# Routed experts that begin after five images' dispatch, with their weights turned inside the MLP and the expert loop written out

## What is computed

```python
h2 = layer_norm(x, norm2_g, norm2_b)
m = gelu(h2 @ W1.T + b1) @ W2.T + b2        # 128 -> 512 -> 128
x = x + m
flat = _ln_t(x)                              # norm again, 8192 x 128
topk_probs, topk_idx = top_k(softmax(flat @ router_w.T), 2)      # 8 experts
h = silu(flat @ w1[e].T) * (flat @ w3[e].T)                      # 128 -> 341
out = sum over the two chosen e of gate * (h @ w2[e].T)
x = x + out
```

## Time and profile before

| what | value |
|---|---|
| median of 3 executions | 1099.61 us (1098.13 to 1100.76) |
| the profiled execution | 1101.17 us, span of the core 1099.4 us |
| blocks up to the MLP | 0 to 427 us |
| MLP steps | 427 to 671 us |
| slot table, rest of the dispatch | 671 to 709 us |
| experts' weights turned | 709 to 724 us |
| expert block, first load to last scatter | 725 to 1054 us |
| last block | to 1099.4 us |
| busy | PE 832.1 (76%), DVE 664.2, ACT 445.1, POOL 447.2 us |
| mean granted clock of PE | 0.886 |

### The profile page before, as it was taken

One profiled execution on the slowest core, in us unless ns is written; L12 is line 12 of the kernel. 1 busy time (PEld: TensorE's weight loads), 2 busy tenths in 40 slices (PEclk: granted clock), 3 DMA queues, 4 the chain that ended last, 5 costly groups with the idle time before them and its releaser, 6 DMA issues. The chain is left out here.

```text
span 1099.4 us, 21202 instructions
## 1 busy us (share of the span) xinstructions
PE 832.1 (76%) x5345; PEld 678.7 (62%) x5346; DVE 664.2 (60%) x2221; ACT 445.1 (40%) x1173; POOL 447.2 (41%) x486
## 2 busy tenths in 40 slices
PE   2798987579999994995667643169998999999920
PEld 1233332468888873884656642159898989888820
DVE  3498887557777755573444233436666666666658
ACT  1233331466666542652443311254343343333335
POOL 0010100255777771035445556404444434444335
PEclk9899999789999996997777755589999999999965
DMA  5010000000000002001012112112111111111159
GB/s 134 25 39 20 19 0 1 1 1 1 2 1 2 2 1 78 25 21 36 30 35 88 40 39 69 48 25 59 57 57 55 58 58 58 58 55 56 58 162 320
DMA packets 60857, 51.99 MB, mean 47 GB/s; under 512 B 9644, under 2 KB 54148, under 8 KB 60804
## 3 DMA queue, kind: packets, MB, share of 16 engines
q1 hardware_dynamic: 41792, 29.49, 9.5%
q0 software_dynamic: 8448, 17.45, 4.4%
q10 hardware_dynamic: 10564, 4.41, 1.4%
HBM read 28.63 MB, written 22.69 MB: 47 GB/s over the span
## 5 line engine op out<-in xcount | busy, mean ns | idle before, releaser
L1646 POOL DMA_INDIRECT mixed<-yt,sidx x136 | 130.2, 957 | 219.7 <-ACT yt L1746 120.9
L1412 POOL DMA_INDIRECT xs<-hx,didx x128 | 124.2, 970 | 152.3 <-DVE didx L1498 107.2
L1695 PE MATMUL bank<-w2T,hmt 128*128 (+1 forms) x816 | 113.3, 275 | 0.0
L559 DVE TENSOR_TENSOR res<-bank,norm 128x512 f32<-128x512 f32 x144 | 95.2, 686 | 25.0 <-PE bank L389 23.2
L1757 DVE TENSOR_TENSOR hm<-bank,sl 128x342 f32<-128x342 f32 x138 | 71.1, 515 | 58.4 <-ACT sl L1728 49.2
L1746 ACT ACTIVATE yt<-bank 128x128 f32<-128x128 f32 x136 | 37.8, 278 | 160.4 <-PE bank L1695 156.7
L1695 PEld LDWEIGHTS bank<-w2T,hmt 128*128 128x128 f32 (+1 forms) x816 | 101.7, 191 | 0.0
L1333 PE MATMUL bank<-downT,mgv 128*128 128x128 f32 x512 | 76.8, 312 | 16.3 <-issue 16.2
L1688 PE MATMUL bank<-cst,hm 128*128 128x128 f32 (+1 forms) x411 | 68.2, 275 | 22.3 <-DVE hm L1757 13.5
L1333 PEld LDWEIGHTS bank<-downT,mgv 128*128 128x128 f32 x512 | 72.3, 225 | 18.8 <-issue 18.5
L458 POOL TENSOR_TENSOR redu<-redu_full,redu 32x512 fp32r<-32x512 f32 x16 | 20.2, 1276 | 148.5 <-ACT redu L432 148.5
(11 more groups left out here) (285 smaller groups left out, 2119.7 us busy)
## 6 DMA issues: line engine op xcount, KB each, us to landing
xg<-xs SPq DMA_DIRECT2D x144, 65.0 KB, 1.8
y<-mixed SPq DMA_DIRECT2D x16, 512.0 KB, 4.8
stage<-in_x SPq DMA_DIRECT2D x8, 512.0 KB, 3.8
out<-tok ACTq DMA_DIRECT2D x16, 256.0 KB, 5.0
mixed<-yt,sidx POOLq DMA_INDIRECT x136, 2.3
raw<-in_L_ffn_w SPq DMA_DIRECT2D x16, 128.0 KB
xs<-hx,didx POOLq DMA_INDIRECT x128
res<-in_L_ffn_w SPq DMA_DIRECT2D x1, 1364.0 KB
```

Of the source, the lines that this page charges most:

```text
L559: dve.tensor_tensor(prod[t].rearrange("p (h w) -> p h w", w=SIDE), tapb[g % TB][:, :].rearrange("p (h w) -> p h w", w=SIDE), norm[s][:, 16 ...
L1412: pool.indirect_dma_start(xs, bass.IndirectOffsetOnAxis(didx[b % NX][:, j, k:k + 1], 0), hx[b % NX][:, j, :], None).then_inc(dispatched[b ...
L1646: pool.indirect_dma_start(mixed, bass.IndirectOffsetOnAxis(sidx[s][:, :], 0), yt[s][:, :], None).then_inc(scattered[s], 16)
L1695: ins = pe.matmul(yb[r % 2][:, 0:P], hmt[r % 2][0:m, k, :], w2T[0:m, c], start=(k == 0), stop=(k == len(HT) - 1))
```

## The change

- **Weights.** The raw weights are loaded during the attention block (SP; POOL clears the padding there), into `raw1` and into the storage of `w2T`. The 24 groups are turned in 12 of the MLP's steps, two each, through the bank that also serves the rows of the router; steps -3 to 2 and 4, 6 to 14. ACT rounds once into the high half, DVE subtracts straight from PSUM (before: two ACT copies, then DVE).
- **MLP.** The gain of the norm is multiplied into the up weights in the set-up and its bias into the up bias, so ACT's copy `hv` goes; `hl` is formed from PSUM. `hx` and `didx` have four buffers instead of two, `hc` two. Both halves of an image are routed in one step (2b+3), with the logits behind the "down" products; ranks come in the step after.
- **Slot table.** It comes before the last step and is formed by small matmuls with constants and a short DVE chain. The slots are ordered so that 73 (`SURE`) come first that hold only rows of images 0 to 4.
- **Dispatch.** POOL dispatches five images in the MLP block. The other three (48 indirect DMAs) come in the expert block: four first, then one ahead of each of 44 scatters. SP waits for five images, and before slot 73 for all.
- **Expert block.** All 136 slots are written out on every engine, with no loop. `yt` and `sidx` have 16 buffers instead of 8.

```diff
-        NX = 2
+        NX = 4
...
-            W_BANKS = 4
+            W_STEPS = (-3, -2, -1, 0, 1, 2, 4, 6, 8, 10, 12, 14)
+            route_of = {2 * b + 3: b for b in range(BATCH)}
+            rank_of = {2 * b + 4: b for b in range(BATCH)}
+            fold_of = {2 * b + 2: b for b in range(BATCH)}
...
+                    def step(n):
+                        if n in W_STEPS:
+                            turn_weights(2 * W_STEPS.index(n))
+                        if has(1):
+                            up(n + 1, 0)
+                        if n in rank_of:
+                            ranks(rank_of[n])
...
+                        if has(0):
+                            down(n)
+                        if route is not None:
+                            logits(2 * route)
+                            logits(2 * route + 1)
...
+                    for n in range(STEP0, STEPS - 1):
+                        step(n)
+                    table()
+                    step(STEPS - 1)
...
-                    for b in range(BATCH):
+                    for b in range(FIRST):
...
+            SURE = FIRST * BT * 2 - (EXPERTS - 1)
...
+                    all_dispatched(FIRST)
+                    for n in range(SLOTS):
+                        if n == SURE:
+                            all_dispatched(BATCH)
+                            sp.wait_ge(filled, 16 * (EXPERTS + 1))
+                        w(sp, "x_turned", n - R)
+                        w(sp, "place_picked", n - R)
...
-                    with pool.Fori(1, SLOTS // R) as i:
-                        for s in range(R):
-                            scatter(i, s)
+                    LEAD = 4
+                    for d in remaining[:LEAD]:
+                        dispatch(pool, *d)
+                    for n in range(SLOTS):
+                        if LEAD + n < len(remaining):
+                            dispatch(pool, *remaining[LEAD + n])
+                        scatter(n)
```

More of the change, by code:

```diff
@@ L1246, in w, with has_of @@
                     eng.wait_ge(S[name], count)
[L1248 to L1252 removed]
+            def has_of(n):
+                return lambda d: 0 <= n + d < CHUNKS
             turnb, upb, downb, backb, small = banks[0], banks[1:5], banks[5], banks[6], banks[7]
@@ L1335, in _, with clear_back @@
-                    w(pe, "set_up", 1)
-                    steps(step)
-                    w(pe, "chosen", BATCH + 1)
-                    pe.matmul(count_out, ones[:, :], ahead[BATCH % 2][:, :], start=True, stop=True).then_inc(S["counted"], 1)
-                    w(pe, "w_loaded", 16 * W_LOADS)
-                    for g, (turns, _, low) in enumerate(groups):
+                    def clear_back(what):
+                        at = BACKS.index(what)
+                        if at:
+                            kind, k = BACKS[at - 1]
+                            if kind == "x":
+                                w(pe, "hc_ready", k + 1)
+                            elif groups[k][2] is not None:
+                                w(pe, "w_low", k + 1)
+                            else:
+                                w(pe, "w_out", k + 1)
```

835 lines of the change are left out of this document (457 added, 378 removed).

## The result

| | median | range | ratio to before |
|---|---|---|---|
| before | 1099.56 us | 1098.13 to 1100.76 | |
| changed | 1106.43 us | 1105.11 to 1109.09 | 1.0067 [1.0051, 1.0084] |

What follows compares the result with a forecast made beforehand. PE was taken to bound the experts, with chains, weights and dispatches costing time before. First scatter at 693 us, plus 119 and 187 us of slots and 46.5 us gave span 1046, median 1045 us; 8-in-10 range 968 to 1087.

Steps and rivals of the forecast that it cites:

- The loop: Expert block: writing it out removes 2.2 us at each of 16 boundaries, 34 us, leaving 2.06 us per undisturbed slot.
- slow stretch: MLP: engines nearly stop some 8 to 11 us into POOL's unbroken dispatch, until about its end; about 11 us per dispatch.
- rival 1: MLP and experts: near-standstill during dispatches mostly goes, being tied to ACT's wait that four buffers remove; 970 us, chance 0.27.
- rival 3: Expert block: straight code is held back whenever POOL issues, 3.2 us per slot, 1171 us, slower than before; chance 0.09.
- The table's 6 us: Between MLP and experts: the slot table takes ten DVE links and five passages through PE, 6 us.
- The loss per dispatch is 10.8 us.: MLP: each image with a dispatch loses 10.8 us over the undisturbed 19.9 us, so 30.7 us per image.
- 8 us for the last step, the gates and the spare rows together: End of the MLP block: last step, gates and SP's spare rows cost 8 us before the experts begin at 679.
- my 665 to 695: Sign that the forecast is right: the experts' first loads come between 665 and 695 us.
- I take 2.7 us per slot, nearest to POOL's own pace.: Expert block: 44 slots that also carry a dispatch take 2.7 us each, 119 us in all.
- rival 2: Expert block: POOL may not be this busy, so 3.8 us for each of 44 slots, 1093 us; chance 0.12.
- The last block stays.: End of the kernel: last scatter to end stays at 46.5 us.
- Four row buffers: nothing.: MLP: ACT no longer waits for the dispatch two images back; costed at nothing, as that wait lies in lost time anyway.

Runs made afterwards that it cites:

- before_unrolled: Kernel before with only its expert block written out, all eight images still dispatched in the MLP: 1062.7 us, ratio to before 0.9649.
- no_dispatch: Changed kernel without the dispatches' indirect writes and the table; experts read constant rows and scatter to fixed places: 981.8 us, ratio to before 0.8906.
- spot_early: Changed kernel with an image's places computed on DVE right behind the residual, ahead of fold: 1119.4 us, ratio to before 1.0203.
- late_spare: Changed kernel with SP's eight spare-row writes moved from the end of the MLP block to slots 24 to 38: 1101.4 us, ratio to before 1.0000.
- all_first: Changed kernel with all eight images dispatched in the MLP and none among the experts: 1084.6 us, ratio to before 0.9841.
- six_spaced: Changed kernel with six images dispatched in the MLP and the rest among the experts, one dispatch per two slots: 1099.9 us, ratio to before 0.9980.
- five_free: Changed kernel with tiny unwaited POOL writes around dispatches, expert dispatches in three of four slots, places ahead of fold, spare-row writes later: 1019.5 us, ratio to before 0.9286.
- gap_free: Changed kernel with four tiny POOL writes, without a wait, after each MLP dispatch: 1042.7 us, ratio to before 0.9503.
- bu_gap2: Kernel before with written-out expert block and two short POOL writes with waits after each MLP dispatch: 1085.8 us, ratio to before 0.9881.
- eight_gap2: Changed kernel with all eight images dispatched in the MLP, two short POOL writes with waits after each dispatch: 1057.1 us, ratio to before 0.9657.

## Why the prediction was wrong

**Right.** The loop: 2.06 us per slot, no boundaries, and 3.5% by itself (before_unrolled). The slow stretch belongs to the dispatch and not to ACT's wait, so rival 1 didn't come. The kernel did get slower, which I had given to rival 3 with 0.09, but not by rival 3's cause: straight code is not held back by POOL at 61%, the slots behind the dispatches take 2.04 us. The table's 6 us came as costed: 685.5 to 691.4.

**"The loss per dispatch is 10.8 us."** I read the loss off two dispatches of the old order and carried it to the new one as a constant. The working is wrong as well: 17.1 us over two dispatches are 8.6 us each, and a share taken off makes it less, not 10.8. That 10.8 lay nearer to the measured loss was luck. no_dispatch puts the image at 21.7 and not 19.9 us, so the loss was 12.3 us, together 3.3 us per image. spot_early shows that it isn't a constant at all: 37.9 - 21.7 = 16.2 us for a burst that starts 4 us earlier in the image. Of the way from image 4's dispatch to the experts, 10.5 us too short in the forecast, 7 are SP's eight writes behind one another (late_spare), which I had put into 8 us for the last step, the gates and the spare rows together. The first load came at 705.8 us, outside my 665 to 695, and PE stood idle for 17.0 us from 690.8 on, over my 15.

**"I take 2.7 us per slot, nearest to POOL's own pace."** This step failed, and by most: 3.36 us, 28.7 of the 57 us. With dispatches out of the block (all_first, no_dispatch) the same slots took 2.06 us. My reason was that a dispatch here can never run far ahead, so that the stretch would end itself. But it doesn't take ten writes in a row: six_spaced lost 1.3 us in each pair of slots, with three writes in a row. My own range for this term ended at 3.2 us and rival 2 stood at 3.8; 3.36 lies between. Rival 2's reason, POOL's busy share, isn't the right one either. In the changed kernel two indirect writes fill 2.53 of 3.36 us, 75%; in five_free seven of them fill 8.8 of 11.0 us, 80%, and PE is busy 137.0 of 153.5 us in it, 89% and not 77%. What is shown is that the dispatches among the scatters cost this. That it is their distance is shown in the MLP (gap_free); here it is only part of the price, 1.3 us against 0.9 us per dispatch. At one dispatch per scatter 1.63 us between writes would itself make 3.26 us per slot.

**"The last block stays."** It got 6 us longer, 5 of them in POOL's drain (2.5 us in the kernel before, 7.7 now). The drain is longer when there are dispatches in the block, but hardly by their number: 6.9 us with 16, 6.8 with 32, 7.7 with 48, and 6.5 with 48 in five_free.

**"Four row buffers: nothing."** No run tests this for the change as it stands. Once the dispatches are kept apart, the old block with two buffers takes 34.4 us per image (bu_gap2) and the new one with four 28.1 us (eight_gap2) at the same 1.72 us per dispatch; the two differ in their order of steps as well.

**The rule.** I went by the rows against the rule of the Trainium skill ("SBUF — State Buffer", the section on the two separate sides) that PE and ACT never wait on anyone. PE's products above took over 10 us instead of 1.85 while POOL's writes were 1.26 us apart, so the rows stand. No run shows that a port of SBUF is what is contended for, and the rule is about ports.

**A cost I had not in the sum.** I priced the new order of steps at 2.5 us per image and took its gains for granted. all_first against before_unrolled shows the new MLP block 2.0% slower than the old one as long as dispatches go out 1.26 us apart: 34.2 against 30.2 us per image. Which part of the new order does it was not tested.

**Left open.** Why a distance of 1.26 us stops the others and 1.63 us doesn't was not settled, nor where between 1.46 us (some images disturbed) and 1.63 us the edge is. Three explanations fall. gap_free excludes that POOL must be made to wait for its own writes. A backlog of the DMA engines isn't it: in the changed kernel's third burst (556 to 577 us) the packets of each write are moved within 0.35 us (one: 0.77 us) and are over before those of the next begin. The profiler isn't it: the unprofiled executions of the changed kernel took 1106.07 to 1109.09 us, the profiled one 1105.11. The fetch of instructions, rival 3's idea, is not excluded, but nothing points to it: its transfers come at anything from 2.6 to 13.3 us into the changed kernel's five bursts, while the standstill begins 11 us into each of them.

In short: the written-out loop brought what was forecast, and two prices of about the same size ate it: the new MLP block under dispatches without distance (2.0%), and dispatches among the scatters (2.3%).

## What to carry to other kernels

Look at the distance of indirect DMAs that GpSimd issues in a row, not at GpSimd's busy share: if matmuls of one group stand 0.7 to 2.1 us apart with "issue" before them during such a run, try something small between the writes, and see first that no engine waits for the dispatch itself (bu_gap2 got slower). Measure a loss in place before moving its cause, for what it costs depends on the work that it falls on. And time the parts of a change apart: here one part won 3.5% and two others lost 2.0% and 2.3%.

## What the runs showed of the hardware

- While POOL issued indirect writes of 128 rows 1.26 us from one another, PE, DVE and ACT nearly stopped from 8 to 11 us into the run, and SP's eight writes took 33.37 us instead of 8.84. At 1.46 us this happened in two images of five, at 1.63, 1.73 and 2.25 us in none of the changed kernel's. Among the experts a dispatch 1.26 us from its neighbours cost 1.3 us, 1.46 us from them 1.1 us, 1.63 us from them 0.9 us.
- POOL's drain at the end of a block took 3.2 us behind 136 scatters of 512-byte rows, and 6.5 to 7.7 us when 16 to 48 dispatches of 520-byte rows were among them.
- SP needed 1.1 us for each pair of a register read from SBUF and a write with that address, when nothing held it up: 8.84 us for eight.
